# Cross attention and quantised linear layer: the preparation's order, the growths' places and the last tile are changed

## What is computed

```python
def reference(x, ctx_512, L0_xattn_Wq, L0_xattn_Wkv_expand, L0_xattn_Wout, L0_ffn_weight):
    # x (8, 1024, 1024) f32, ctx (8, 64, 256), 16 heads of 64
    def _L0_xattn_ref(q, latent_kv, Wq, Wkv_expand, Wout):
        qp = q @ Wq.T
        k, v = jnp.split(latent_kv @ Wkv_expand.T, 2, axis=-1)
        scores = jnp.einsum('bhqd,bhkd->bhqk', qh, kh) * inv_sqrt_d
        scores = jnp.where(causal, scores, jnp.finfo(scores.dtype).min)
        attn = jax.nn.softmax(scores, axis=-1)
        out = jnp.einsum('bhqk,bhkd->bhqd', attn, vh)
        return out.transpose(0, 2, 1, 3).reshape(b, sq, H) @ Wout.T
    def _L0_ffn_ref(x, weight):
        w_fp8, w_scale = _quant_e4m3(weight)     # scale = amax / 448, over the whole tensor
        x_fp8, x_scale = _quant_e4m3(x2d)
        return _scaled_mm(x_fp8, w_fp8.T, x_scale, w_scale)
    x = x + _L0_xattn_ref(_layernorm(x), ctx_512, L0_xattn_Wq, L0_xattn_Wkv_expand, L0_xattn_Wout)
    x = x + _L0_ffn_ref(_layernorm(x), L0_ffn_weight)
```

## Time and profile before

| | |
|---|---|
| median of 3 runs | 1822.14 us (1821.7 to 1823.01) |
| profiled execution | 1823.34 us, span 1821.5 us |
| mean granted TensorE clock | 0.987 of full |
| TensorE busy | 1747.5 us, 96% |
| VectorE busy | 1341.1 us, 74% |
| ScalarE busy | 691.2 us, 38% |
| GpSimd busy | 187.2 us, 10% |
| DMA | 263.96 MB, mean 145 GB/s |

### The profile page before, as it was taken

The page is one execution under the profiler, slowest core; times in us unless marked ns, Lnnn a source line. Parts: engine busy times, 40 slices in busy tenths (PEclk is TensorE's granted clock), DMA queues, the critical chain, the costliest instruction groups (busy, mean ns, idle before and its releaser), DMA issues.

```text
span 1821.5 us, 26733 instructions
## 1 busy us (share of the span) xinstructions
PE 1747.5 (96%) x10730; PEld 840.7 (46%) x10730; DVE 1341.1 (74%) x1839; ACT 691.2 (38%) x644; POOL 187.2 (10%) x143
## 2 busy tenths in 40 slices
PE   7689999999999999999999999999999999799998
PEld 4434454445444544454445444544454444355554
DVE  6776678667866777777777777777777664777775
ACT  6632233223322332233223322332233221688886
POOL 0000000000000000000000000000000020355555
PEclk9899999999999999999999999999999999899999
DMA  9665535553545344545453545454544443677763
GB/s 316 157 180 132 127 96 115 135 135 94 116 130 142 93 116 127 133 105 113 130 134 104 119 124 133 105 119 125 134 104 107 127 114 116 256 274 266 267 239 138
DMA packets 371545, 263.96 MB, mean 145 GB/s; under 512 B 322304, under 2 KB 324864, under 8 KB 370944
## 3 DMA queue, kind: packets, MB, share of 16 engines
q1 hardware_dynamic: 371456, 262.71, 52.7%
HBM read 119.28 MB, written 71.30 MB: 105 GB/s over the span
## 4 chain that ended last, share of the span: by engine, by line
issue 89%; POOL 9%; PE 1%; DVE 0%; POOLq 0%; ACT 0%; DMA 0%; DVEq 0%
POOL m_buf L519 4%; POOL tile_space L519 3%; POOL rstd_x L502 1%; PE ps_all L559 1%; POOL rstd L512 1%; DVE amax L992 0%; DMA tile_space<-in_ctx_dram 0%; POOLq L506 0%; POOL amax_all L497 0%; DVE tile_space L986 0%; ACT tile_space L757 0%; PE ps_all L539 0%; POOLq L518 0%; ACT wo_t L762 0%; PE ps_all L549 0%
## 5 line engine op out<-in xcount | busy, mean ns | idle before, releaser
L607 PE MATMUL ps_all<-m_buf,tile_space 128*128 128x512 f16 x3072 | 679.3, 380 | 4.7 <-DVE wo_t L1200 4.7
L607 PE MATMUL ps_all<-n_buf,tile_space 128*128 128x512 f16 x3024 | 671.1, 379 | 0.0
L607 PEld LDWEIGHTS ps_all<-m_buf,tile_space 128*128 128x128 f16 x3072 | 298.8, 98 | 372.2 <-issue 14.2
L607 PEld LDWEIGHTS ps_all<-n_buf,tile_space 128*128 128x128 f16 x3024 | 291.6, 98 | 345.1 <-issue 3.3
L732 PE MATMUL ps_all<-wo_t,tile_space 128*128 128x512 bf16 x1024 | 233.4, 381 | 0.8 <-DVE tile_space L1303 0.8
L828 ACT ACTIVATE tile_space<-tile_space,neg_mean 128x1024 f32<-128x1024 f32 x63 | 72.4, 1149 | 293.0 <-DVE neg_mean L1100 293.0
L824 ACT ACTIVATE tile_space<-tile_space,score_scale 128x1024 f32<-128x1024 f32 x64 | 73.5, 1148 | 281.2 <-DVE tile_space L1070 281.2
L502 POOL TENSOR_TENSOR rstd_x<-veps_x,minus_half 128x1 f32<-128x1 f32 x64 | 35.3, 551 | 1406.5 <-DVE veps_x L1043 1406.5
L732 PEld LDWEIGHTS ps_all<-wo_t,tile_space 128*128 128x128 bf16 x1024 | 98.0, 98 | 107.8 <-issue 1.9
L1074 DVE TENSOR_REDUCE hsum<-tile_space 128x16 f32<-128x1024 f32 x64 | 78.1, 1220 | 77.8 <-ACT tile_space L824 77.8
L820 ACT ACTIVATE tile_space<-tile_space 128x1024 f16<-128x1024 f32 x64 | 67.6, 1057 | 175.6 <-DVE tile_space L1080 175.6
(11 more groups left out here) (125 smaller groups left out, 1694.3 us busy)
## 6 DMA issues: line engine op xcount, KB each, us to landing
tile_space<-in_x_dram SPq DMA_DIRECT2D x128, 512.0 KB, 3.8
x_scratch<-tile_space SPq DMA_DIRECT2D x64, 512.0 KB, 2.9
m_buf<-x_scratch SPq DMA_DIRECT2D x32, 512.0 KB, 4.0
tile_space<-x_scratch SPq DMA_DIRECT2D x32, 512.0 KB, 4.0
out_dram<-m_buf SPq DMA_DIRECT2D x32, 512.0 KB, 2.9
out_dram<-tile_space SPq DMA_DIRECT2D x32, 512.0 KB, 2.9
m_buf<-in_L_xattn_Wq_dram SPq DMA_DIRECT2D x4, 1024.0 KB, 11.2
n_buf<-in_L_xattn_Wout_dram SPq DMA_DIRECT2D x2, 2048.0 KB, 18.5
```

What stands on the lines that cost most here:

```text
L607: mm = nc.tensor.matmul(to[:, cols], left[:, ls, c * P:(c + 1) * P], right[:, rs, c, cols], start=(c == 0 and i == 0), stop=(c == CT - 1 a ...
```

## The change

What it does, part by part:

- **Scales.** The scales of keys and values no longer come from their maxima but from bounds: largest context value times the largest row sum of absolute Wkv (wkv_sums), reduced by GpSimd. Keys and values are split straight from PSUM (split_kv_hi, split_kv_lo), with an order of PSUM slots written by hand (ORDER0). Wkv's turned copy, the split keys and the split values lie in other buffers.
- **Wq.** It is split into wq_stack itself, unstacked: upper halves in even places, lower in odd. The first key matrix is made from that by first_m, 48 matmuls of 64 columns and 64 rows a chunk; chunks 0 and 1 before the first scores, chunk c+2 within the wait of chunk c of the scores of tile 0. Afterwards SP stores three quarters of wq_stack, 1024 KB each from 64 partitions, to a scratch in DRAM and loads them back to their stacked places (store_wq, restack_wq); the key chunks of batch 1 wait for that.
- **Output weight.** It is split in natural order, the even blocks on VectorE, the odd on GpSimd, and turned by eight DMA transposes. Its scale comes from the maximum, of which ScalarE contributes sums for four blocks. Batch 0's pairs of n_buf wait for all eight; they stand at chunks 4, 6 and 8 of the scores of tile 1, and the fourth in output product 0.
- **x.** Tiles 0 and 1 are loaded between the weights and normalised during the preparation.
- **Growths.** Key chunks 0 and 1 stand in the scores of step 6, the others in its output product with two gaps; the first pair of the next n_buf stands in the output product of step 7, the others in the scores of step 0. Output products go through n_buf in the order in which it grows (n_block). The operations of ScalarE and VectorE are placed to match.
- **Gap.** Four of the eight transposes of the second weight (turn_w8, 616) follow the last output product; the deviation's power is taken for the last tile alone, the others earlier; the first two values are made by VectorE.
- **End.** The last tile is scaled by ScalarE, added by VectorE (not GpSimd) and stored in two halves of columns.
- The maxima of the second weight stand in steps 4 and 5 instead of 5 and 7.

```diff
-        AMAX_AT = {(0, 5): (0, 1), (0, 7): (2, 3), (1, 5): (4, 5), (1, 7): (6, 7)}
+        AMAX_AT = {(0, 4): (0, 1), (0, 5): (2, 3), (1, 4): (4, 5), (1, 5): (6, 7)}
...
-        PAIRS_AT = (0, 3, 6, 8)
+        def n_block(c):
+            return c % 2 * QUAD + c // 2
+        FIRST_PAIRS_AT = {4: 0, 6: 1, 8: 2}
+        PAIRS_AT = {0: 1, 5: 2, 8: 3}
+        NEXT_PAIR_AT = 2
+        KEYS_AT_S = {3: 0, 6: 1}
+        KEYS_AT_O = {1: (2,), 2: (3,), 4: (4,), 6: (5,), 7: (6,), 8: (7,)}
...
-            for i in range(4):
-                sp.wait_ge(wq_split, i + 1)
-                move_wq(i)
+            def store_wq(i):
+                e, rows = ((0, ODD), (1, EVEN), (1, ODD))[i]
+                sp.dma_start(wq_dram[i], wq_heads(e)[rows]).then_inc(wq_out, 16)
+            def restack_wq(i):
+                e, rows = ((1, ODD), (0, ODD), (1, EVEN))[i]
+                sp.dma_start(wq_heads(e)[rows], wq_dram[i]).then_inc(wq_back, 16)
...
+            def turn_wout(a):
+                sp.wait_ge(wout_lo[a % 2], a // 2 + 1)
+                sp.dma_start_transpose(wo_blocks[:, :, a * P:(a + 1) * P], wout_split[a]).then_inc(wout_turned, 16)
...
+            for a in range(2, CT):
+                turn_wout(a)
+            sp.wait_ge(kv_stored, 128)
+            load_x(xr, got_xr, 0, 0)
+            for s, src in enumerate(k_split):
+                sp.dma_start(kv_dram[s, :, 0:NP, :], src).then_inc(k_stored, 16)
+            for k in range(2):
+                sp.wait_ge(grow_full[k], QUAD)
+            for i in range(3):
+                store_wq(i)
+            sp.wait_ge(k_stored, 32)
             sp.wait_ge(p_lo, 1)
             turn_p(0, 0)
             sp.dma_start(w8_raw[:], Wffn.rearrange("(a p) c -> p a c", p=P)).then_inc(got_w8, 16)
+            sp.wait_ge(wq_out, 48)
+            for i in range(3):
+                restack_wq(i)
...
+            def scale_wout(a):
+                nc.gpsimd.tensor_scalar(wout_f[:, a, :], wout_f[:, a, :], to_f16[:, 2:3], None,
+                                        ALU.mult).then_inc(wout_scaled, 1)
...
+            def first_m(ct):
+                to = grow_ps[ct % 2]
+                if ct >= 2:
+                    pe.wait_ge(grow_free[ct % 2], ct // 2)
+                for j in range(NP):
+                    for i, (ws, ks) in enumerate(PASSES):
+                        for k, rows in enumerate((EVEN, ODD)):
+                            cols = to[:, (k * NP + j) * SK:(k * NP + j + 1) * SK]
+                            mm = nc.tensor.matmul(cols, wq_nat[ws][rows, j, ct * P:(ct + 1) * P],
+                                                  k_split[ks][rows, j, 0:SK],
+                                                  start=(i == 0), stop=(i == len(PASSES) - 1))
+                mm.then_inc(grow_full[ct % 2], 1)
...
+            def first_chunk(c):
+                pe.wait_ge(grow_free[c % 2], c // 2 + 1)
+                if c + 2 < CT:
+                    first_m(c + 2)
+            split_product(ps_s, xt_buf[0], m_buf, s_full, ready=first_chunk)
...
+            act.wait_ge(sum_ready, T - 2)
+            for k in range(2):
+                cols = slice((1 - k) * HALF, (2 - k) * HALF)
+                act.wait_ge((y_half, y_full)[k], (1, T)[k])
+                nc.scalar.activation(y_t[1][:, cols], y_ps[1][:, cols], ACT.Copy,
+                                     scale=small[:, 8:9]).then_inc(y_part, 1)
...
+            def first_values(t):
+                dve.wait_ge(got_x1[t], 16)
+                nc.vector.tensor_scalar(v_t[t], x2[t], quant_a[:, t:t + 1], quant_b[:, t:t + 1], ALU.mult,
+                                        ALU.add).then_inc(v_first, 1)
```

More of the change, by code:

```diff
@@ L528, in next_slot @@
                 use[0] += 1
-                if n >= 4:
-                    pe.wait_ge(turned_read, n - 3)
-                return slots0[n % 4]
+                before = EARLIER0[n]
+                if before in KV_USES:
+                    pe.wait_ge(kv_read, KV_USES.index(before) + 1)
+                elif before is not None:
+                    pe.wait_ge(turned_read, sum(k not in KV_USES for k in range(before + 1)))
+                return SLOTS0[n]
             pe.wait_ge(const_made, 6)
@@ L1139, in step @@
                     variance(t + 2, e)
-                if here:
-                    grow_n(2)
-                    grow_n(3)
-                if not (known and t == 0):
+                if not first:
                     peak(t - 1, 1 - e)
@@ L1146, in step @@
                     normalise(t + 2, e)
-                if here:
+                if grow:
+                    grow_m(0)
+                if here and not first:
                     grow_n(4)
@@ L1151, in step @@
                     x_low(t + 2, e)
-                if here:
-                    grow_n(6)
-                    grow_n(7)
-                piece = QUANT_AT.get((b, tt))
+                if first:
+                    for c in range(4):
+                        grow_n(c)
+                if grow:
+                    grow_m(1)
                 if piece is not None:
@@ L1163, in step @@
                         maxima(t + 1)
+                if first:
+                    grow_n(4)
+                    grow_n(5)
+                if here:
+                    grow_n(6)
+                    grow_n(7)
+                if next_n:
+                    take_n(0, uses(b + 1, 1, 0))
+                if not known or t + 1 < T:
                     sums(t + 1)
-                grow = is_step(tt, TB - 2) and not last
                 if grow:
-                    grow_m(0)
+                    grow_m(2)
+                if next_n:
+                    take_n(1, uses(b + 1, 1, 1))
                 if not known or t + 1 < T:
@@ L1174, in step @@
                 if grow:
-                    for c in range(2, CT):
+                    for c in range(4, CT):
                         grow_m(c)
```

590 lines of the change are left out of this document (350 added, 240 removed).

## The result

The change is slower: 1829.86 us (median of 5 runs) against 1822.14 in the same session, a ratio of 1.0045 with the interval 1.003 to 1.0059. The profiled execution has a span of 1828.1 us, against 1821.5 before; its parts say where the 6.6 us lie.

The account below looks back on a forecast made before the run. TensorE, busy 96% of the span, was taken as the bound, so only its idle and slow-clock time could be won. From 1822.14 us, +10.0 - 13.5 - 2.9 - 2.2 = -8.6 gave 1813.5, range 1798 to 1827.

Parts of the forecast that it names:

- Preparation, SP queue: Transposes and Wq's transfers in one queue delay tile 2's scores from 127.5 to 135.3; with slow clock, preparation costs +10.0 us.
- these scores at about 135: Sign of being right: the scores of tile 2, at the preparation's end, start at about 135 us.
- Rival 2: Wq's stores and loads in the preparation run at 411 GB/s: -12.7 us, total 1801; chance 0.25.
- rival 4: Preparation: transposes in a row don't overlap, eleven on the path add 23 us, total 1837; chance 0.12.
- rival 5: Preparation: transposes in a row move at the load's rate, 1.3 us each, -14 us, total 1800; chance 0.02.
- rival 3: Spreading only moves the growth stalls (1823), or transposes cost 3.4 us each (1822): no change; chance 0.16.
- Preparation, compute side: VectorE's 48 us of work from about 5 empties the first bank at 55; tile 1's scores start near 78, 14 us won.
- GpSimd also waits for ScalarE's halves in between; the last block is done near 75 ...: no cost: Preparation: GpSimd's share of the output weight's split, eight operations of 2.13 us from about 52.6, delays no transpose.
- My upper bound for this term, +22.8: The preparation's worst case: transposes at 3.4 us each and the chain 4 us later.
- Batch boundaries: At seven boundaries, waits of 17.0 us in all shrink to 0.5 each: -13.5 us, bounds -8 and -17.
- Gap: Between the kernel's halves, fewer small transposes, a one-column power, reordered scales and first value on VectorE: -2.9 us, worst -1.5.
- End: Last tile finished in two halves, with a VectorE add and shorter store: -2.2 us, bounds -1.2 and -2.6.

Follow-up runs that it names:

- e5: The changed kernel with Wq's stores moved to steps 0, 1 and 2 and its loads back to steps 2, 3 and 4 of batch 0: 1802.19 us.
- e7: e6 with the next batch's eight key loads behind step 0's transposes and Wq's first store moved from step 0 to step 1: 1788.23 us.
- e9: The changed kernel with only the next batch's eight key loads moved from the start of step 0 to its end: 1826.62 us.
- e4: e1 plus e2's edit, and the output weight's odd blocks scaled and split on ScalarE and VectorE instead of GpSimd: 1808.92 us.
- e6: e4 with Wq's stores and loads in e5's steps: 1791.91 us.
- e8: The kernel before with only the change's places of pairs and key chunks, and of the second weight's maxima: 1803.2 us, ratio 0.9889.
- e1: The changed kernel with Wq's three stores and three loads back moved out of the preparation into steps 1 to 5 of batch 0: 1819.29 us.
- e2: The changed kernel with tile 0's normalising, its power included, moved behind GpSimd's two reductions across partitions: 1824.94 us.

## Why the prediction was wrong, step by step

- **Preparation, SP queue: right in kind and nearly in size.** Wq moves at 217 and 209 GB/s, taken as 225; transposes in a row took 2.49 us each (12.45 / 5), taken as 2.6. Wq's six transfers, 28.0 us in my sum, gave back 27.7 (e5). From the output weight's landing to output product 0 it is 23.7 us (102.51 to 126.16), forecast 23. From there to tile 2 it is 30.4 (to 156.59), forecast 25.3: "eight key loads, 512 KB at 225: 2.3" was too small by 1 to 2 (e7 and e9 give 3 to 4), Wq's loads at 209 GB/s add 1, and the other 2 to 3 are not taken apart. Of the signs I named for being right, idle time ahead of output 0, more ahead of tile 2, the rate in the two stretches, waits under 5 us at the pairs (2.4) and an end 1.9 us nearer are there; "these scores at about 135" is not. The Trainium skill (SBUF — State Buffer, Door 1: The DMA port swizzle) had it that 64 partitions reach half the ports; the trace now agrees for transfers between DRAM and 64 partitions as well. Rival 2 is out by this, rivals 4 and 5 by the 2.49, rival 3 by the 2.4 us of waits left. The result is slower than before, to which I gave 0.14, nearly all of it for rival 4; it came by another way.
- **Preparation, compute side: the step that failed.** I summed VectorE's work to 48 us and let "it starts with the context's landing", so that the first bank is emptied at 55 (5 and 48 are 53; 2 us have no term). The work was right (47.5 us by the rows, waits left out), the assumption that VectorE never waits was not: it waited 9.60 us for GpSimd's first power, and the first take of the keys' matrix came at 63.8, 8.8 late. Tile 1's scores were 13.2 late (91.2 for 78): behind the first bank VectorE waited 4.19 us more, for ScalarE, which waited 5.98 for a block that GpSimd scales.
- **"GpSimd also waits for ScalarE's halves in between; the last block is done near 75 ...: no cost": failed.** I priced its operations at 2.13 us each and let them start at 52.6. They cost 2.8 to 3.8 for a scaling, but above all started at 67.7. VectorE's scale was ready at 61.1; the rest is the standstill of 7.42 behind the reduction at 59.9. The second transpose waited for that, and so did the key chunks.
- These two make the output weight land at 102.5 instead of 87: +15.5. With +0.7 and +5.1 in the queue behind it and +0.7 more slow clock (13.45 - 10.52 = 2.9 us, forecast 2.2) that is the 22.0 us by which this term was missed. The experiments return most of it, not all. With both standstills off the path the output weight lands at 90.2 to 90.6 in e4, e6 and e7, 12 of the 15.5 us, and the totals fall by 10.3 and 10.4. e7 comes near to my own dates: first transpose 60.3 (58.6), tile 1's scores 80.8 (78), output weight 90.2 (87), output 0 102.9 (99, where the pairs would allow it). The 3 us left of the 15.5, and some of the 5.1 behind output 0, no run explains.
- My upper bound for this term, +22.8, stretched transposes and "the chain 4 us later"; no bound covered an engine that stands still between two kinds of instruction. Before, GpSimd goes from a reduction (52.49) to a power (66.22) as well, but waits 13.36 us for VectorE there, so no row named the standstill.

```profile
52.49 0.37 POOL L505 PARTITION_ALL_REDUCE amax_all<-amax  x1 [19.09 <-DVE amax L1204]
66.22 0.60 POOL L502 TENSOR_TENSOR rstd_x<-veps_x,minus_half 128x1 f32<-128x1 f32 x1 [13.36 <-DVE veps_x L1043]
```

- **Batch boundaries: -19.1 for -13.5.** The remainder per boundary was as worked out (0.34 for 0.5). The forecast gain was too small because I took it from the waits view, which lists 17.0 us; short stalls are not in it. (e8 has 18.6. The 0.5 more in the change are three transposes of the second weight, 0.45 each, that left this stretch, less 0.8 of longer waiting at its end, 4.24 for 3.42.) Here is TensorE before, at the key chunks of batch 1: undisturbed, chunks follow at 2.23 us.

```profile
243.69 1.46 PE L607 MATMUL ps_all<-n_buf,tile_space 128*128 128x512 f16 x6
245.92 1.46 PE L607 MATMUL ps_all<-n_buf,tile_space 128*128 128x512 f16 x6
248.71 1.46 PE L607 MATMUL ps_all<-n_buf,tile_space 128*128 128x512 f16 x6
251.26 1.46 PE L607 MATMUL ps_all<-n_buf,tile_space 128*128 128x512 f16 x6
```

The intervals 2.79, 2.55 and the next, 2.35, are 1.0 us over in all, of which the view lists 0.39. Seven times 0.6 is 4 us. The period would have shown it. From one batch's first pair to the next one's it is 182.04 us before (829.78 to 1011.82) and 179.74 after (1023.39 to 1203.13), so 2.3 us each for seven boundaries, and 1.1 more for the first two, where the maxima stood (183.3): 18.3 us.
- **Gap: -4.5 for -2.9.** The mechanisms gave what was asked: from the last residual's half on VectorE to the first magnitude 7.94 before and 6.54 after, from there to the first rounding operation 2.41 and 1.25. Together 2.6 us, forecast 2.45 without the small transposes, whose 0.45 lies ahead of this stretch. The other 1.9, for which I had no term, go with the clock: TensorE's last output product took 13.21 us at a granted clock of 0.79 and takes 12.22 at 0.86, and from its first transpose behind the gap to the third it needed 9.7 at 0.66 and needs 8.8 at 0.73. These are the rows of GpSimd, ScalarE and VectorE after the earlier trace rows.

```profile
1563.59 0.56 POOL L569 TENSOR_TENSOR rstd<-var,minus_half 128x1 f32<-128x1 f32 x1 [12.41 <-DVE var L1422]
...
1567.08 2.34 ACT L1032 ACTIVATE ps_all<-m_buf,ident 128x1024 f32<-128x1024 f32 x2 [2.33 <-DVE ident L1449]
...
1568.33 1.23 DVE L1465 SCALAR_TENSOR_TENSOR n_buf<-ps_all,n_buf 128x1024 f32<-128x1024 f32 x1 [0.43 <-ACT ps_all L1032]
```

- **End: -1.9 for -2.2.** Both halves took 0.69 (forecast 0.65 and 0.75).

```profile
1823.53 0.69 ACT L1076 ACTIVATE tile_space<-ps_all,small 128x512 bf16<-128x512 f32 x1 [0.98 <-PE ps_all L821]
...
1824.25 0.69 DVE L1505 TENSOR_TENSOR tile_space<-tile_space 128x512 f32<-128x512 f32 x1 [0.31 <-ACT tile_space L1076]
```

The rivals were all about transfers and stalls of the kind already seen; none held an engine that stands still with nothing to wait for, and that is where a chance was missing. Not settled: why the first standstills of a launch (10 to 11 us) are longer than the later ones (6 to 8).

## What to carry to other kernels

A bulk transfer that isn't needed soon should stand where its queue has slack, never ahead of a transpose that an engine waits for; but give it the deadline of its first reader, or the wait only moves (e1). When a sum of an engine's work is used as a date, ask of each operation in its row which other engine must answer first, and put those with slow answers behind the rest. And price stalls from the period of the loop, not from the list of waits.

## What the runs showed of the hardware

- GpSimd stood still at each change between a reduction across partitions and ordinary operations that no longer wait for another engine covered: 9.99, 10.95, 6.12 and 7.42 us in the changed kernel, 7.83, 7.68 and 7.74 in e2, with no instruction in the record. Where it would have waited anyway (11.64 us for VectorE, and then the power 0.1 us behind its operand) it costs nothing. The Trainium skill (GPSIMD Engine Reference, 2.1 Instruction dispatch) tells of about 6 us of code loading at the first call of a freshly loaded kernel, without a visible instruction. The standstills here, 6.1 to 11 us, are that long or longer, and they came back with each later change of kind. That they are the same thing is not shown.
- The DMA engines moved 512 KB transposes in a row at 204 GB/s over 11 us, half of the 395 of a plain store from 128 partitions.
